# Long convolution packed into column and row tiles, with the sequence as weight and its result fetched by DMA

## The chip, the core and the metric

One core of one Trainium2 chip. The time is device microseconds for one execution, the median of three runs. Names used here: TensorE (PE; PEld are its weight loads), VectorE (DVE), ScalarE (ACT), GpSimd (POOL), SyncE (SP), which issues most DMAs. Arithmetic is in fp32. F32R is the format in which TensorE reads 4-byte values in one pass with reduced precision; the kernel gets full precision from it by splitting an operand into a high and a low part and adding three products.

## The reference

A block of two layers on x of 2 × 4096 × 256. The first normalises the rows, projects them to 3 × 256 channels, applies a 3-tap convolution along the sequence, and then a convolution as long as the sequence, whose filter is a sum of 16 decaying exponentials per channel:

```python
x2, x1, v = jnp.split(z_pre, 3, axis=1)
h = jnp.sum(residues[:, :, None] * jnp.exp(log_poles * t[None, None, :]), axis=1)
xv = x1 * v
yconv = jnp.fft.irfft(jnp.fft.rfft(xv, n=n) * jnp.fft.rfft(h, n=n)[None], n=n)[..., :Lc]
y = (yconv + xv * D_skip[None, :, None]) * x2
y = y.transpose(0, 2, 1) @ out_proj_w.T + u
zm = rmsnorm(y, post_norm_w)
return y + jax.nn.gelu(zm @ l1_w.T) * (zm @ l2_w.T) @ l3_w.T
```

The second layer is a feed-forward of width 1024 whose two weights get, per batch of 4096 rows, an update made from a few of its input rows.

## The kernel before

Three stages, each a block of its own per engine. The instructions of each engine stand in the order written; semaphores are the only link between engines.

**Stage A** (`phase_a`) takes 16 units of 512 rows: normalisation, projection, short convolution. It writes x2 to DRAM (`x2_scratch`) and leaves xv = x1·v, turned so that time within a chunk of 128 is the partition, in `seq` [time 128, channel 256, chunk 64] (`gate_rows`, L376). It also makes the first 128 filter taps per channel and writes them to `taps_scratch`. `scan_consts` (L254) makes the masks `own` and `later` on GpSimd.

**Stage B** (`phase_b`) is the long convolution, in 32 groups of 8 channels. Per group:

- TensorE `states_of`: the weighted sums of each chunk into 8 × 16 states. The weights are `collect`, exponentials of the poles; `seq` streams. Both are split into F32R parts by ScalarE (`gather`, L672 to L677) and VectorE (`low_parts`, L719), so three products of 512 columns (L749).
- VectorE: `inflow` masks and scales the sums (L729), and a scan over the chunks carries the states (L735, 512 columns), with ScalarE's `decay` (L681).
- TensorE: the part within a chunk is a product with a Toeplitz matrix of the taps, one per channel: the 128 × 128 matrix is the weight, the channel's 64 columns of `seq` stream, in plain fp32 (L762). The part from the earlier chunks is `spread` (L684) as weight and `state` streamed, 512 columns (L768), added in the same PSUM bank `ps_y`.
- ScalarE `take` (L693) copies the result back to `seq`, over its input.
- SyncE loads the Toeplitz matrices of a group straight from `taps_scratch` (512 KB, runs of 512 B) into one of two buffers. GpSimd meanwhile loads and splits the weights of stage C, one piece after another through one buffer `raw`.

TensorE's order is: sums of group g + 1, Toeplitz product of g, state product of g. The engines' steps run in a loop over pairs of groups (`run_steps`), with addresses in registers.

**Stage C** (`phase_c`) takes 32 units of 256 rows through output projection, MLP, feed-forward and norms, as a software pipeline. For the convolution's result, GpSimd copies a unit's two chunks out of `seq` (`copy_y`, L948), TensorE turns them by four transposes into `ps_rt` between blocks 2 and 3 of the MLP (`turn_y`), and VectorE multiplies by x2 there (`gate_y` part 0, L1117), then splits the product (`yt`) for the output projection. The same PSUM tile `ps_rt` serves the two other turns of a unit. TensorE's products are written through one helper, so its matmuls of C all have L1331 and its transposes L1341.

## Time and profile before

| | |
|---|---|
| median of 3 runs | 1200.15 us (1199.13 to 1202.2) |
| the profiled execution: its time, its span | 1203.2 us, 1201.5 us |
| TensorE busy, share of the span | 1123.1 us, 93% |
| VectorE, ScalarE, GpSimd busy | 957.5, 757.2, 325.9 us |
| stage A, B, C | to about 206, to about 326, to the end |
| mean granted clock of TensorE | 0.979 of full speed |
| moved by DMA | 80.72 MB, mean 67 GB/s |

A time in a row below is counted from the start of the span. Matmuls are pipelined, so the distance between two starts says more than the length of one. A count (x16) on a row of the timeline means that so many instructions were merged into it, and the row's time is from the first start to the last end.

### The profile page before, as it was taken

Reading aid. Unit: us, or ns where it says so; the run is one execution under the profiler, and the core shown is the slowest. Engines: PE = TensorE matmul, PEld = TensorE weight load, DVE = VectorE, ACT = ScalarE, POOL = GpSimd, SP = SyncE. Lnnn points to the kernel's source line nnn. Section 1 sums busy time; section 2 is a strip of 40 time slices with the busy share of each in tenths; the row PEclk is TensorE's granted clock in tenths of the full one; section 3 lists DMA queues with packets and bytes.
Section 4 is the critical chain, followed back from the end, with each engine's and each line's share of the span. In section 5 each row is a group of like instructions: output and inputs, shape, how many; then the busy total and the mean of one; then the engine's idle time right before and its main releaser. Section 6 shows DMA issues by size and latency. Waiting matters only on the chain.

```text
span 1201.5 us, 25905 instructions
## 1 busy us (share of the span) xinstructions
PE 1123.1 (93%) x9056; PEld 1079.9 (90%) x9056; DVE 957.5 (80%) x2375; ACT 757.2 (63%) x1697; POOL 325.9 (27%) x587
## 2 busy tenths in 40 slices
PE   3999998899868899999999999998999999999996
PEld 3889997678668899999999999997999999999996
DVE  5999997998647978877788878789788777888774
ACT  5878886677544656665566665566566655666643
POOL 5676663640011121112211122221211122211111
PEclk9999999999978899999999999998999999999999
DMA  3232322765432011111111111141111111111000
GB/s 115 79 115 77 100 71 72 238 180 157 132 114 71 27 37 45 45 45 46 36 36 51 39 45 45 37 141 36 36 45 45 45 45 37 37 45 45 28 19 27
DMA packets 90837, 80.72 MB, mean 67 GB/s; under 512 B 5040, under 2 KB 85584, under 8 KB 90720
## 3 DMA queue, kind: packets, MB, share of 16 engines
q1 hardware_dynamic: 89184, 76.76, 20.4%
q0 software_dynamic: 672, 2.39, 0.6%
q8 instruction: 68, 1.11, 0.4%
q14 instruction: 49, 0.40, 0.1%
q10 hardware_dynamic: 864, 0.05, 0.0%
HBM read 62.12 MB, written 17.07 MB: 66 GB/s over the span
## 4 chain that ended last, share of the span: by engine, by line
PE 51%; ACT 9%; issue 7%; DVE 5%; POOL 1%; ACTq 0%; POOLq 0%; DVEq 0%
PE ps_ring L1331 23%; PE ps_w L1331 13%; PE ps_m L1331 8%; PE ps_o L1331 3%; PE ps_rt L1341 3%; ACT gate L1021 2%; ACT frow L1028 2%; ACT pt_h L1015 2%; ACT ht_h L1040 1%; ACT hid L1043 1%; DVE base L1186 1%; POOL sc L953 1%; DVE ht_l L1108 1%; PE ps_m L1382 1%; DVE bn L1096 1%
## 5 line engine op out<-in xcount | busy, mean ns | idle before, releaser
L953 POOL TENSOR_TENSOR sc<-sc,neg_half 128x2 f32<-128x2 f32 x128 | 95.8, 749 | 673.2 <-DVE sc L1286 385.7
L1021 ACT ACTIVATE gate<-ps_ring 128x256 f32<-128x256 f32 x192 | 72.8, 379 | 168.1 <-PE ps_ring L1331 167.2
L1331 PE MATMUL ps_ring<-mt_h,wl_h 128*128 128x256 f32 x640 | 133.5, 291 | 6.4 <-ACT mt_h L1085 6.4
L1331 PE MATMUL ps_ring<-mt_l,wl_h 128*128 128x256 f32 x640 | 131.4, 287 | 6.7 <-DVE mt_l L1108 6.7
L1331 PE MATMUL ps_ring<-mt_h,wl_l 128*128 128x256 f32 x640 | 130.0, 285 | 0.0
L1043 ACT ACTIVATE hid<-ps_ring,b1s 128x256 f32<-128x256 f32 x256 | 111.5, 483 | 17.1 <-DVE ht_l L1108 17.0
L1134 DVE TENSOR_TENSOR prod<-ps_ring,gate 128x256 f32<-128x256 f32 x192 | 80.4, 419 | 46.1 <-ACT gate L1021 44.6
L1331 PE MATMUL ps_ring<-xt_h,we_h 128*128 128x256 f32 x512 | 106.1, 288 | 8.1 <-ACT hid L1043 5.8
L1331 PEld LDWEIGHTS ps_ring<-mt_h,wl_h 128*128 128x128 f32 x640 | 101.6, 197 | 7.7 <-ACT mt_h L1085 4.4
L1331 PEld LDWEIGHTS ps_ring<-mt_l,wl_h 128*128 128x128 f32 x640 | 101.7, 196 | 7.6 <-DVE mt_l L1108 7.6
L1108 DVE TENSOR_TENSOR ht_l<-hid,ht_h 128x256 fp32r<-128x256 f32 x256 | 100.8, 422 | 6.1 <-ACT hid L1043 1.7
L1331 PEld LDWEIGHTS ps_ring<-mt_h,wl_l 128*128 128x128 f32 x640 | 101.3, 196 | 0.0
L1331 PE MATMUL ps_ring<-xt_l,we_h 128*128 128x256 f32 x512 | 101.2, 279 | 0.0
L1331 PE MATMUL ps_ring<-xt_h,we_l 128*128 128x256 f32 x512 | 101.1, 278 | 0.0
L432 DVE SCALAR_TENSOR_TENSOR conv<-ps_z,sw,conv 128x512 f32<-128x512 f32 x128 | 92.1, 740 | 4.8 <-ACT conv L367 3.9
L1331 PEld LDWEIGHTS ps_ring<-xt_h,we_h 128*128 128x128 f32 x512 | 77.2, 188 | 14.7 <-ACT hid L1043 11.3
L1108 DVE TENSOR_TENSOR pt_l<-prod,pt_h 128x256 fp32r<-128x256 f32 x160 | 87.7, 548 | 1.1
L502 PE MATMUL ps_z<-zt_h,win_h 128*128 128x258 f32 x384 | 84.0, 300 | 2.8 <-DVE zt_l L427 2.7
L1000 ACT ACT_TABLE_LOAD x64 | 82.1, 1283 | 1.1
L502 PE MATMUL ps_z<-zt_h,win_l 128*128 128x258 f32 x384 | 78.2, 285 | 0.0
L502 PE MATMUL ps_z<-zt_l,win_h 128*128 128x258 f32 x384 | 78.2, 285 | 0.0
L1331 PEld LDWEIGHTS ps_ring<-xt_h,we_l 128*128 128x128 f32 x512 | 77.8, 188 | 0.0
(179 smaller groups left out, 3061.9 us busy)
## 6 DMA issues: line engine op xcount, KB each, us to landing
toep<-taps_scratch SPq DMA_DIRECT2D x32, 512.0 KB, 3.8
xa<-in_x SPq DMA_DIRECT2D x16, 512.0 KB, 4.6
x_scratch<-x2c SPq DMA_DIRECT2D x16, 512.0 KB, 3.5
x2s<-x_scratch SPq DMA_DIRECT2D x32, 256.0 KB, 2.9
xa_c<-in_x SPq DMA_DIRECT2D x32, 256.0 KB, 2.7
xb_c<-in_x SPq DMA_DIRECT2D x32, 256.0 KB, 2.7
out<-frow SPq DMA_DIRECT2D x32, 256.0 KB, 2.1
base<-in_w SPq DMA_DIRECT2D x8, 256.0 KB, 4.4
```

The source lines that it names most:

```text
L432: nc.vector.scalar_tensor_tensor(conv_of(m, u), tap_of(b, tap), sw[:, m, tap:tap + 1], conv_of(m, u), ALU.mult, ALU.add).then_inc(S[done], 1)
L502: mm = nc.tensor.matmul(slot(b)[:, a, 0:HALF + HALO], win_r[w][:, k, m * P:(m + 1) * P], zt[r][:, u % 2, k, cols], start=(j == 0), stop=(j ...
L953: nc.gpsimd.tensor_tensor(sc[:, to], sc[:, to], neg_half[:, 0, 0:CC], ALU.pow).then_inc(S[done], 1)
L1000: nc.scalar.activation(mark_act[:], neg_half[:, 0, 0:1], function)
L1015: nc.scalar.activation(high, src, ACT.Copy).then_inc(S["ph_done"], 1)
L1021: nc.scalar.activation(gate[rows_of, m % 2], ring[m % RING][rows_of, 0], ACT.Gelu_apprx_tanh).then_inc(S["gate_done"], 1)
L1028: nc.scalar.activation(frow[:, c], frow[:, c], ACT.Identity, scale=sc[:, 2, c:c + 1], bias=shift[:, 2, c:c + 1]).then_inc(S["f_norm"], 1)
L1043: nc.scalar.activation(hid[:, m % HIDS], block_of, ACT.Gelu, bias=b1s[:, m:m + 1]).then_inc(S["hid_done"], 1)
L1108: nc.vector.tensor_tensor(low, src, high.bitcast(F32), ALU.subtract).then_inc(S[done], 1)
L1134: nc.vector.tensor_tensor(product_views(m)[1], value, gated, ALU.mult).then_inc(S["prod_done"], 1)
L1331: mm = nc.tensor.matmul(out, lhs(a, kk), rhs(b, kk), start=(j == 0), stop=(closed and j == len(todo) - 1))
L1341: mm = nc.tensor.transpose(dst[:, b, chunk(c)], src[:, c, b * P:(b + 1) * P], ident[:])
```

## The change

- The layout of `seq` becomes [128, channel mod 128, channel half, chunk]: channels p and p + 128 lie side by side as a pair. Poles, residues and taps are put in the same order. A group is four pairs.
- Chunk sums: no split. For each pair a plain fp32 matmul with 32 weight columns writes its own 32 partitions of `ps_s` (column tiles of 32), 128 columns streamed. Both channels of a pair meet both channels' poles; `own` zeroes the wrong half, and `inflow`, `decay` and the scan have 256 columns in place of 512. One exponential makes `collect` for four groups.
- Toeplitz product: the sequence is the weight (64 columns), the Toeplitz matrix streams (128 columns). The two channels of a pair write partitions 0 to 63 and 64 to 127 (column tiles of 64). The result has the chunk as partition and time as column.
- State product: `state` is the weight (64 rows, 128 columns) and `spread` streams, in row tiles of 64 that write two banks.
- Three Toeplitz buffers in place of two; the poles come in two pieces (832 KB and 1 MB) in place of three; `raw` has two buffers; the loops are written out.
- Stage C fetches the result: for each unit four DMAs, each from one partition of `seq` (128 runs of 512 B) to the 128 partitions of `yin`. `copy_y` and `turn_y` go, and `gate_y` reads `yin`. SyncE asks for unit n + 2 once the gate of unit n + 1 has read the buffer, and ahead of the load of x2.

Stages A and B, cut:

```diff
+        yin = sb(whole, "yin", [P, KB, TC])
         mark = sb(whole, "mark", [P, 1])
...
-        seq = sb(whole, "seq", [P, D, COLS])
+        seq = sb(whole, "seq", [P, P, KB, COLS])
...
-                    sp.dma_start(taps_dram.rearrange("(k p) t -> p k t", p=P), taps[:]
+                    sp.dma_start(taps_dram.rearrange("(p k) t -> p k t", k=KB), taps[:]
...
+                nc.gpsimd.memset(own[:], 1.0).then_inc(v["bconst"], 1)
+                nc.gpsimd.memset(own_high[:], 1.0).then_inc(v["bconst"], 1)
+                nc.gpsimd.memset(later[:], 1.0).then_inc(v["bconst"], 1)
+                pool.wait_ge(v["bconst"], 5)
+                nc.gpsimd.memset(later[:, :, :, 0:1], 0.0).then_inc(v["bconst"], 1)
...
-                nc.scalar.activation(seq[:, j * P:(j + 1) * P, u * CA:(u + 1) * CA],
+                nc.scalar.activation(seq[:, :, j, u * CA:(u + 1) * CA],
...
         lpb = sb(ctx, "lpb", [P, (GROUPS - FIRST) * P])
         pole_chunk = sb(ctx, "pole_chunk", [P, GROUPS])
-        collect = sb(ctx, "collect", [P, 2, P])
-        collect_r = [sb(ctx, f"collect_{s}", [P, 2, P], F32R) for s in "hl"]
-        seq_r = [sb(ctx, f"seq_{s}", [P, 2, GC * COLS], F32R) for s in "hl"]
+        collect = sb(ctx, "collect", [P, 2, QUAD * P])
         spread = sb(ctx, "spread", [P, 2, CH])
-        decay = sb(ctx, "decay", [P, 2, 2 * GC * BC])
-        inflow = sb(ctx, "inflow", [P, 2, 2 * GC, BC])
-        state = sb(ctx, "state", [P, 2, 2 * GC * BC])
-        toep = sb(ctx, "toep", [P, 2, GC, CH])
-        raw = sb(ctx, "raw", [P, KB, FF])
+        decay = sb(ctx, "decay", [P, 2, 2 * KB * B * BC])
+        inflow = sb(ctx, "inflow", [P, 2, 2, KB * COLS])
+        state = sb(ctx, "state", [P, 2, 2, KB * COLS])
+        toep = sb(ctx, "toep", [P, TOEPS, GC, CH])
+        raw = sb(ctx, "raw", [P, 2, KB, FF])
         post = sb(ctx, "post", [P, KB])
-        ps_s = [ps(ctx, f"ps_s{i}", [P, 2 * GC, BC]) for i in range(2)]
-        ps_y = [ps(ctx, f"ps_y{i}", [P, 2 * GC * BC]) for i in range(2)]
...
+        ps_s = [ps(ctx, f"ps_s{i}", [P, KB * COLS]) for i in range(2)]
+        ps_y = [ps(ctx, f"ps_y{i}", [P, 2, 512]) for i in range(2)]
...
-            def load(g, par):
+            def load(g):
 
                 src = bass.AP(taps_dram.tensor, 2 * CH * GC * g, [[1, P], [2 * CH, GC], [1, CH]])
-                wait(sp, toep_mm, g - 1)
-                sp.dma_start(toep[:, par], src).then_inc(toep_in[par], 16)
+                wait(sp, toep_mm, g - TOEPS + 1)
+                sp.dma_start(toep[:, g % TOEPS], src).then_inc(toep_in[g % TOEPS], 16)
...
+            load(0)
+            load(1)
             load_poles(0)
-
-            def step(g, par, k):
-                if not (is_step(g) and g == 0) and valid(g + 1, GROUPS):
-                    load(g + 1, 1 - par)
-                if is_step(g) and g in (1, 2):
-                    load_poles(g)
-
-            run_steps(sp, step, plan)
+            load(2)
+            load_poles(1)
+            for g in range(3, GROUPS):
+                load(g)
             for i in range(2):
                 sp.wait_ge(v["x2_out"][i], 16 * UA // 2)
             sp.dma_start(v["x2s"][:], v["x2_dram"][:, :, 0:TC]).then_inc(v["x2_in"], 16)
+            sp.wait_ge(y_done, GROUPS)
             sp.wait_ge(v["x2_in"], 16)
 
...
+            def load(k, dst, src):
+                pool.dma_start(dst, src).then_inc(raw_in[k % 2], 16)
+
+            def load_l(k, w):
+                load(k, raw[:, k % 2], w.rearrange("(k p) f -> p k f", p=P))
+
+            raw_out = raw[:, 0, :, 0:D]
+            raw_l3 = flat(1)[:, 0:FULL * D].rearrange("p (m o) -> p m o", o=D)
+            raw_stack = raw[0:3 * REST, 0, 0, 0:D]
+            pool.dma_start(post[:], v["post_w"]).then_inc(post_in, 16)
+            load_l(0, v["l2_w"])
+            load_l(1, v["l1_w"])
+            pool.wait_ge(post_in, 16)
+            count = 0
+            for k, (dst, at) in enumerate(((v["wl2"], 0), (v["wl1"], REST))):
...
+                if k == 0:
+                    load(0, raw_out, v["out_w"].rearrange("(k p) o -> p k o", p=P))
+                else:
+                    load(1, raw_l3, v["l3_w"][0:FULL * P].rearrange("(m p) o -> p m o", p=P))
...
+                    for q in range(3):
+                        load(0, raw_stack[q * REST:(q + 1) * REST], v["l3_w"][FULL * P:])
...
+            def gather(q):
+
+                wait(act, s_mm, QUAD * (q - 1))
+                first = q * QUAD
+                if q == 0:
+                    nc.scalar.activation(collect[:, 0, 0:FIRST * P], lpb_first[:], ACT.Exp, scale=to_end[:, 0:1]
+                                         ).then_inc(collect_done, 1)
+                    act.wait_ge(poles_more[0], 16)
+                    nc.scalar.activation(collect[:, 0, FIRST * P:], lpb[:, 0:(QUAD - FIRST) * P], ACT.Exp,
+                                         scale=to_end[:, 0:1]).then_inc(collect_done, 1)
+                else:
+                    if (first - FIRST) * P + QUAD * P > pole_pieces[1]:
+                        act.wait_ge(poles_more[1], 16)
+                    at = (first - FIRST) * P
+                    nc.scalar.activation(collect[:, q % 2], lpb[:, at:at + QUAD * P], ACT.Exp,
+                                         scale=to_end[:, 0:1]).then_inc(collect_done, 1)
+
+            def powers(g):
+                wait(act, scan_done, g - 1)
+                nc.scalar.activation(decay[:, g % 2], later[:].rearrange("p a c j -> p (a c j)"), ACT.Copy,
+                                     scale=pole_chunk[:, g:g + 1]).then_inc(decay_done, 1)
+                wait(act, y_mm, g - 1)
+                nc.scalar.activation(spread[:, g % 2], ahead[:], ACT.Exp, scale=lpg[:, g:g + 1]
+                                     ).then_inc(spread_done, 1)
+
+            def take(g):
+                act.wait_ge(y_mm, g + 1)
+                nc.scalar.activation(seq[:, pairs_of(g)].rearrange("p (r a) k c -> p r (a k c)", r=2),
+                                     ps_y[g % 2][:, :, 0:2 * P], ACT.Copy).then_inc(y_done, 1)
+
             nc.scalar.activation(pole_chunk[:], lpg[:], ACT.Exp, scale=float(CH)).then_inc(pole_done, 1)
+            gather(0)
             act.wait_ge(pole_done, 1)
...
+            powers(0)
+            gather(1)
+            for g in range(GROUPS):
                 if valid(g + 1, GROUPS):
-                    powers(g + 1, 1 - par)
+                    powers(g + 1)
                 if valid(g - 1, GROUPS):
-                    take(g - 1, 1 - par)
-
-            run_steps(act, step, plan)
-            take(GROUPS - 1, 1)
+                    take(g - 1)
+                if g % QUAD == 0 and 2 <= g // QUAD + 1 < GROUPS // QUAD:
+                    gather(g // QUAD + 1)
+            take(GROUPS - 1)
...
-            def low_parts(g, par):
-                dve.wait_ge(high_done, 2 * (g + 1))
-                for low, src, high in ((seq_r[1], seq[:, bass.ds(g * GC, GC), :].rearrange("p h c -> p (h c)"),
-                                        seq_r[0]), (collect_r[1], collect[:, par], collect_r[0])):
-                    nc.vector.tensor_tensor(low[:, par], src, high[:, par].bitcast(F32), ALU.subtract
-                                            ).then_inc(low_done, 1)
-
-            low_parts(0, 0)
-            low_parts(1, 1)
...
+            for g in range(GROUPS):
                 dve.wait_ge(s_mm, g + 1)
                 wait(dve, scan_done, g - 1)
-
-                nc.vector.scalar_tensor_tensor(inflow[:, par, :, 1:BC], ps_s[par][:, :, 0:BC - 1],
-                                               rg[:, bass.ds(g, 1)], own[:, :, 0:BC - 1],
+                ends = ps_s[g % 2][:, 0:KB * COLS - 1].unsqueeze(1).broadcast_to([P, 2, KB * COLS - 1])
+                nc.vector.scalar_tensor_tensor(inflow[:, g % 2, :, 1:], ends, rg[:, g:g + 1],
+                                               own[:].rearrange("p a c j -> p a (c j)")[:, :, 0:KB * COLS - 1],
                                                ALU.mult, ALU.mult).then_inc(inflow_done, 1)
                 dve.wait_ge(inflow_done, g + 1)
                 dve.wait_ge(decay_done, g + 1)
                 wait(dve, y_mm, g - 1)
-                nc.vector.tensor_tensor_scan(state[:, par], decay[:, par],
-                                             inflow[:, par].rearrange("p c j -> p (c j)"), 0.0,
+                nc.vector.tensor_tensor_scan(state[:, g % 2].rearrange("p a c -> p (a c)"), decay[:, g % 2],
+                                             inflow[:, g % 2].rearrange("p a c -> p (a c)"), 0.0,
                                              ALU.mult, ALU.add).then_inc(scan_done, 1)
...
-            def states_of(g, par):
-                pe.wait_ge(low_done, 2 * (g + 1))
+            def states_of(g):
+                pe.wait_ge(collect_done, 1 if g < FIRST else 2 + g // QUAD)
                 wait(pe, inflow_done, g - 1)
-                for j, (a, b) in enumerate(((0, 0), (0, 1), (1, 0))):
-                    mm = nc.tensor.matmul(ps_s[par][:].rearrange("p c j -> p (c j)"),
-                                          collect_r[a][:, par], seq_r[b][:, par],
-                                          start=(j == 0), stop=(j == 2))
+                for j in range(PAIRS):
+                    at = (g % QUAD) * P + j * 2 * STATES
+                    mm = nc.tensor.matmul(ps_s[g % 2][j * 2 * STATES:(j + 1) * 2 * STATES],
+                                          collect[:, g // QUAD % 2, at:at + 2 * STATES],
+                                          seq[:, g * PAIRS + j].rearrange("p k c -> p (k c)"),
+                                          start=True, stop=True)
                 mm.then_inc(s_mm, 1)
...
-            def step(g, par, k):
+            def out_of(g, j):
+                return ps_y[g % 2][:, j // 2, (j % 2) * P:(j % 2 + 1) * P]
+
+            states_of(0)
+            for g in range(GROUPS):
                 if valid(g + 1, GROUPS):
-                    states_of(g + 1, 1 - par)
-                pe.wait_ge(toep_in[par], 16 * (k + 1))
+                    states_of(g + 1)
+                pe.wait_ge(toep_in[g % TOEPS], 16 * (g // TOEPS + 1))
                 wait(pe, y_done, g - 1)
-                for c in range(GC):
-                    mm = nc.tensor.matmul(ps_y[par][:, c * COLS:(c + 1) * COLS], toep[:, par, c],
-                                          seq[:, bass.ds(g * GC + c, 1), :].rearrange("p h c -> p (h c)"),
-                                          start=(c == 0), stop=False, skip_group_check=True)
+                for j in range(PAIRS):
+                    for k in range(KB):
+                        mm = nc.tensor.matmul(out_of(g, j)[k * HALF:(k + 1) * HALF],
+                                              seq[:, g * PAIRS + j, k], toep[:, g % TOEPS, KB * j + k],
+                                              start=(j % 2 == 0), stop=False, skip_group_check=True)
                 mm.then_inc(toep_mm, 1)
                 pe.wait_ge(spread_done, g + 1)
                 pe.wait_ge(scan_done, g + 1)
-                nc.tensor.matmul(ps_y[par][:], spread[:, par], state[:, par], start=False, stop=True,
-                                 skip_group_check=True).then_inc(y_mm, 1)
-
-            run_steps(pe, step, plan)
+                for a in range(2):
+                    for r in range(2):
+                        rows = slice(r * HALF, (r + 1) * HALF)
+                        mm = nc.tensor.matmul(out_of(g, 2 * r + a), state[rows, g % 2, a], spread[rows, g % 2],
+                                              start=False, stop=(a == 1), skip_group_check=True)
+                mm.then_inc(y_mm, 1)
```

Stage C and the order of the channels, cut:

```diff
+            def load_y(n):
+                for k in range(KB):
+                    for c in range(CC):
+                        row = k * COLS + n * CC + c
+                        sp.dma_start(yin[:, k, c * CH:(c + 1) * CH],
+                                     seq[row:row + 1].rearrange("p i k c -> p i (k c)")).then_inc(S["y_in"], 16)
+
+            load_y(0)
...
                 if valid(n + 2, UC):
+                    sp.wait_ge(S["yf_done"], n + 2)
+                    load_y(n + 2)
                     sp.wait_ge(S["yl_done"], n + 2)
                     sp.dma_start(x2s[:], x2_dram[:, :, (n + 2) * TC:(n + 3) * TC]).then_inc(S["x2_in"], 16)
...
-            def copy_y(n):
-
-                wait(pool, S["yt_mm"], n)
-                nc.gpsimd.tensor_copy(ys[:], seq[:, :, n * CC:(n + 1) * CC].rearrange("p h c -> p c h")
-                                      ).then_inc(S["y_copied"], 1)
-
...
-                    dve.wait_ge(S["yt_mm"], n + 1)
+                    dve.wait_ge(S["y_in"], 16 * KB * CC * (n + 1))
                     dve.wait_ge(S["x2_in"], 16 * (n + 1))
-                    back = ps_t[:].rearrange("p b (c t) -> p (b c) t", t=CH)[:, :, ::-1]
+                    back = yin[:].rearrange("p b (c t) -> p (b c) t", t=CH)[:, :, ::-1]
...
-            def turn_y(n):
-                pe.wait_ge(S["y_copied"], n + 2)
-                wait(pe, S["zl_done"], n)
-                transpose_unit(ps_t, ys).then_inc(S["yt_mm"], 1)
-
...
-                pe.wait_ge(S["yf_done"], n + 1)
+                wait(pe, S["zl_done"], n)
...
-                pe.wait_ge(S["yf_done"], min(u + 3, UC))
...
+    grouped = np.arange(D).reshape(KB, GROUPS, GC // KB).transpose(1, 2, 0).reshape(D)
```

## Rows read from the trace of the kernel before

**Rows 1.** windows by stage: each engine busy (instructions), granted clock, DMA share, GB/s

```profile
226.00:326.00 100.00, 96.73 (x599) 76.76 (x598) 84.16 (x108) 68.67 (x162) 22.93 (x20) 1.00 0.56 165
...
332.00:343.00 11.00, 6.38 (x29) 5.86 (x29) 1.98 (x4) 5.14 (x12) 0.72 (x1) 0.50 0.74 237
...
430.00:790.00 360.00, 356.85 (x3063) 353.98 (x3063) 287.13 (x828) 222.95 (x536) 70.52 (x126) 1.00 0.14 45
```

**Rows 2.** timeline, TensorE in stage B: start us, us, engine, line, operation

```profile
227.16 1.08 PE L768 MATMUL ps_y<-state,spread 128*128 128x512 f32 x2
...
264.61 0.80 PE L749 MATMUL ps_s<-seq_h,collect_h 128*128 128x512 f32 x1
...
265.48 0.39 PE L749 MATMUL ps_s<-seq_h,collect_l 128*128 128x512 f32 x1
265.71 1.89 PE L762 MATMUL ps_y<-seq,toep 128*128 x16
267.44 1.08 PE L768 MATMUL ps_y<-state,spread 128*128 128x512 f32 x2
267.95 0.79 PE L749 MATMUL ps_s<-seq_h,collect_h 128*128 128x512 f32 x1
...
323.68 1.08 PE L768 MATMUL ps_y<-state,spread 128*128 128x512 f32 x2
```

**Rows 3.** timeline around the transposes of one unit in stage C

```profile
599.50 0.40 PE L1331 MATMUL ps_ring<-mt_l,wl_h 128*128 128x256 f32 x2
...
599.73 0.60 PE L1341 MATMUL ps_rt<-ident,ys 128*128 128x128 f32 x4
...
600.40 0.39 PE L1331 MATMUL ps_ring<-mt_h,wl_l 128*128 128x256 f32 x2
...
600.69 1.10 DVE L1108 TENSOR_TENSOR pt_l<-prod,pt_h 128x256 fp32r<-128x256 f32 x1
...
602.67 0.39 PE L1331 MATMUL ps_ring<-mt_l,wl_h 128*128 128x256 f32 x2
602.89 0.39 PE L1331 MATMUL ps_ring<-mt_h,wrest_h 128*64 128x256 f32 x2
603.12 0.39 PE L1331 MATMUL ps_ring<-mt_l,wrest_h 128*64 128x256 f32 x2
...
625.32 0.60 PE L1341 MATMUL ps_rt<-ident,ys 128*128 128x128 f32 x4
```

**Rows 4.** groups of stage B (busy us, mean ns | idle before); one timeline row

```profile
L735 DVE TENSOR_TENSOR_SCAN state<-decay,inflow 128x512 f32<-128x512 f32 x32 | 40.2, 1257 | 1.1
...
L729 DVE SCALAR_TENSOR_TENSOR inflow<-ps_s,rg,own 128x496 f32<-128x496 f32 x32 | 23.3, 730 | 9.9 <-PE ps_s L749 9.9
L681 ACT ACTIVATE decay<-later,pole_chunk 128x512 f32<-128x512 f32 x32 | 22.6, 708 | 0.0
L674 ACT ACTIVATE seq_h<-seq 128x512 fp32r x26 | 16.0, 615 | 0.0
...
L693 ACT ACTIVATE seq<-ps_y 128x512 f32 x26 | 15.0, 576 | 0.0
...
L684 ACT ACTIVATE spread<-ahead,lpg 128x128 f32<-128x128 f32 x32 | 12.8, 401 | 26.7 <-PE ps_y L768 26.6
...
220.23 2.25 DVE L735 TENSOR_TENSOR_SCAN state<-decay,inflow 128x512 f32<-128x512 f32 x1
```

**Rows 5.** one microsecond of stage B with the DMA engines full

```profile
230.00:231.00 1.00, 1.00 (x11) 1.00 (x11) 0.96 (x2) 1.00 (x4) 0.00 (x0) 1.00 0.96 314
```

**Rows 6.** DMA issues: count, KB each, median us to landing

```profile
toep<-taps_scratch SPq DMA_DIRECT2D x32, 512.0 KB, 3.8
...
x2s<-x_scratch SPq DMA_DIRECT2D x32, 256.0 KB, 2.9
```

**Rows 7.** timeline at the start of stage C

```profile
325.66 0.39 SPq L903 DMA_DIRECT2D xa_c<-in_x  x1
...
327.19 0.69 DVE L1117 TENSOR_TENSOR x2s<-ps_rt,x2s 128x512 f32<-128x512 f32 x1 [5.82 <-PE ps_rt L1341]
```

167 lines of the change are left out of this document (49 added, 118 removed).

## Prediction

> **What bounds the kernel now.** TensorE is busy for 93% of the span, so I read the busy time by stage first [rows 1]. The long convolution (stage B) lies at 206 to 326 us, and the row-wise stage C fills the rest. From 226 to 326 TensorE is busy 96.7 of 100 us, in steady C 356.9 of 360. The reader should see three more things there. The DMA engines are at 0.56 in B and only at 0.14 in C. ScalarE has 69 of 100 us of work in B. And TensorE's granted clock is 1.00 (2.4 GHz) in both, and 0.50 (1.2 GHz) at the seam at 332 to 343, behind a stretch in which it stood still.
>
> Then I read one group of 8 channels of B in order of time [rows 2]. A group takes 267.95 − 264.61 = 3.34 us, and its parts follow one another. The 16 records of the Toeplitz product go from 265.71 to 267.44: 1.73, so 0.108 each. The state product starts at 267.44 and has two records of 512 columns. The record behind it shows 0.79 where its twin shows 0.39, so its first 0.40 were waiting, and the state product held the engine until 268.35: 0.91 us for 1024 columns, 0.89 ns a column. The three records of the chunk sums have the remaining 0.70. A record of these, in F32R, starts 0.23 ahead of the next one (265.48, 265.71) for 512 columns: 0.45 ns a column. So a plain fp32 product is two records, each at twice the time per column of an F32R one. 1.73 + 0.91 + 0.70 is all of the 3.34: B is TensorE's own work, with no wait of size. Over the last 28 groups the mean is (323.68 − 227.16)/28 = 3.45, since some waited.
>
> In C the result of B costs TensorE four transposes per unit of 256 rows. The pair of matmuls ahead of them starts at 599.50, the second pair after them at 600.40. Between lie two pairs' own time, 603.12 − 602.67 = 0.45 us [rows 3]. 0.90 − 0.45 leaves 0.45 us for the transposes.
>
> **Stage B, part by part.** *TensorE.* A record of 128 plain fp32 columns costs 128 × 0.89 ns = 0.114 us. After the change a group has 4 matmuls of 128 columns for the chunk sums (8 records), 8 for the Toeplitz product (16) and 4 for the states (8): 32 records, 3.65 us if nothing overlaps. That is 0.31 more than now, since the Toeplitz product streams 128 columns where it streamed 64. So everything hangs on whether the tiles run beside each other, and no row of before shows two tiles at once. The nearest are the 128*64 matmuls of C: alone in their half of the array they start 0.23 a pair, like the full ones, and the change of shape costs nothing that can be seen (602.67, 602.89, 603.12) [rows 3]. The bounds are 3.65 (no overlap) and, with four tiles at once for the sums and two for the rest, 0.23 + 0.91 + 0.46 = 1.6.
>
> I choose between them like this. The two records of one fp32 matmul share a tile and must follow each other. If records start in program order, the second of one tile runs with the first of the next, which is a factor of two for every part, four tiles or not: 1.83. Weight loads come on top. A Toeplitz record of today streams 64 columns, 0.057 us, but they start 0.108 apart, so a load of 128 weight columns sets their pace. The state product of after has 8 such loads, 0.87 in place of 0.46. That gives 2.24; I take 2.2 us a group.
>
> *VectorE* loses both low parts; its inflow shrinks from 496 to 254 columns and its scan from 512 to 256. Even unchanged the two are 0.73 + 1.26 = 2.0 [rows 4], halved about 1.2. *ScalarE* loses the high parts; decay (0.71, on half the columns), spread (0.40), take (0.58) and a quarter of one exponential on 512 columns (0.61/4) are at most 1.84 [rows 4]. Both are below 2.2.
>
> *DMA.* Each group still reads 512 KB of Toeplitz rows. With the engines full, one microsecond shows 314 GB/s [rows 5], so 524 kB take 1.7 us. A load took 3.8 us to land [rows 6]. With three buffers three periods must hold that and about 0.9 of Toeplitz product: 1.6 us a group. The DMA floor of 1.7 is near, yet below 2.2.
>
> *The start of B.* ScalarE now waits, in order, for an 832 KB piece of poles before it makes the first decay and spread, where 192 KB sufficed. Queued by then are two Toeplitz loads, that piece, and GpSimd's two 672 KB loads, which now leave together: 3.3 MB, over 10 us at 0.31 MB/us. Behind the waiting ScalarE stand VectorE's first scan, TensorE's first state product and all later groups. But the queue itself sets the fourth group: four Toeplitz loads, 1.9 MB of poles and GpSimd's 1.4 MB are 5.4 MB, 17 us from 207, which ends at 224, and the fourth group's state product of before started at 227.16 [rows 2]. I cost the start at nothing, with −2 to +3. GpSimd's splits once held a scan for 2.25 us [rows 4]; with shorter groups that reaches TensorE. I add 2 us.
>
> B: 28 × (3.45 − 2.2) − 2 = 33 us saved. At the DMA floor 28 × 1.75 − 2 = 47.
>
> **Stage C.** Taking the transposes out gives 0.45 us in each of 31 units, 13.9 us. They lie on the path that sets the end, for TensorE hardly waits here and what it does wait for (ScalarE's gates and hidden layer) follows from its own blocks. A low part at 600.69 takes 1.10 us beside GpSimd's copy [rows 3], more than the product needs alone; that is VectorE's time, which is not the path in the steady part. I do not add it.
>
> What comes in is four SyncE DMAs of 64 KB per unit, each from one partition to 128. In the steady part they leave when the gate of the unit before has read the buffer and have nearly a period, 625.32 − 599.73 = 25.6 us [rows 3], to land. That period is their cover. Behind them on SyncE's queue are the loads of x2, the store of the result and the two loads of x, each for the next unit; I take them as covered while the four take less than half a period. The first transfer has no cover: the first gate starts at 327.19 today, 1.5 us after the stage's first issue at 325.66 [rows 7]. Below: two or three issues of 0.4 us and 2.9 us, as 256 KB of x2 took to land [rows 6]; together 2 more than now. Above: if one partition gives only what one of 16 DMA engines gets at 314 GB/s, 19.6 GB/s, 64 KB take 3.3 us and four 13.4, 12 more than now. The row is as far from this as can be, so I take the middle, 7.
>
> By "SBUF — State Buffer", Door 1, of the Trainium skill, one SBUF port passes about 27 GB/s to DMA, and neighbouring partitions share a port. Four loads of 2.4 us would be an estimate of 9.6, and this term 9 in place of 7. No trace here has a load from one partition.
>
> **The sum.** −33 − 14 + 7 = −40. The profiled execution took 1203.2 (span 1201.5), so 1163. It lies 3.05 above the median of the runs: 1160. Stage A changes in the stride of its writes to seq (runs of four elements, as before) and in some GpSimd constants made once; I cost both at nothing, with GpSimd's idle time in A as cover, and at 2 us without it.
>
> **The rivals.** *Tiles overlap only in part* (0.18). A Toeplitz weight load of 64 columns is half of 0.108. If such loads are not hidden behind the neighbour's stream, 16 add 0.87 to 2.24, and half of that if every second one is. A group is then 2.7 to 3.1, B saves 19 to 8, the total is −26 to −15: about 1180. Against it: the full-width loads of C hide, since a pair of 256 columns takes no more than its columns at 0.45 ns. For it: the Toeplitz records of today are paced by loads.
> By "TensorE: Matmul & The Clock Gate", Part 3, of the Trainium skill, a weight load overlaps running matmuls only where the row groups differ, and column tiles share theirs; the rows of C do not agree with it in that plain form, and no row of before has two tiles.
>
> *No overlap at all* (0.12), the case on the other side. The place is the Toeplitz step. A group becomes 3.65 and 0.05 of gaps: 32 × 0.36 = 12 us slower. With −14 and +7 that is +5: 1205. It decides from 3.5 us a group on. For it: nothing in this trace shows two tiles at once. Against it: only that their operands and results lie apart.
>
> *The single-partition loads become C's bound* (0.08). When four take over 25 us the gate waits in every unit; at 6.7 us each the 1.5 us a unit eats all that B gave, which is 1200. The upper bound above is half of that.
>
> *Packed, as forecast*, has 0.62 and a range of its own, 1141 to 1171: below, B at the DMA floor and the first transfer at +2 (−47 − 14 + 2 = −59); above, 2.4 us a group and the first at +12 (−27 − 14 + 12 = −29). The full range is 1140 to 1190: it takes in most of the partial case and leaves out the last two. What a measurement tells from no change is 0.3%, 3.6 us. Faster are the packed and the partial case and half of the loads' case: 0.83. Within 0.3% are 0.05 of what is left, where the small terms decide. Slower: 0.12.
>
> **What would show it.** Right: groups of B 2.2 us apart; Toeplitz records of the two halves less than 0.1 apart, with the clock at 1.00; units of C shorter by 0.45; the first gate of C 4 to 14 us after the stage begins. Wrong: records 0.11 apart and a period of 3.7; TensorE waiting in every group for toep (then the DMA queue is the bound, not the array) or for state; the clock at 0.50 within B, for each record then takes twice its time; or the gate waiting for yin in every unit.

## The result, and the profile after

| | before | after |
|---|---|---|
| median of the runs | 1200.08 us (1199.13 to 1202.2, 4 runs) | 1170.78 us (1164.41 to 1173.5, 4 runs) |
| the profiled execution: its time, its span | 1203.2, 1201.5 us | 1170.21, 1168.5 us |
| mean granted clock | 0.979 | 0.966 |

The ratio is 0.9746, with a 95% interval of 0.9704 to 0.9788: faster, by 29 us, where 40 were forecast (1160, range 1140 to 1190). Four runs of the changed kernel lie 9 us apart, those of before 3.

Windows by stage come first, as for before [rows 1]; the cuts are the first Toeplitz load (start of stage B), the first load of stage C and its first gate.

```profile
0.00:210.61 210.61, 182.38 (x1408) 173.66 (x1408) 176.29 (x309) 158.19 (x275) 130.18 (x278) 0.98 0.26 85
210.61:299.44 88.83, 70.25 (x1024) 52.80 (x1024) 42.22 (x66) 46.65 (x106) 26.84 (x26) 0.87 0.84 248
299.44:310.04 10.60, 0.00 (x0) 0.00 (x0) 0.00 (x1) 0.00 (x0) 0.00 (x0) 0.68 0.64 54
310.04:1168.50 858.46, 815.86 (x6848) 804.70 (x6848) 661.77 (x1936) 516.68 (x1228) 128.18 (x256) 0.98 0.34 57
```

Before, stage B began at 206.5 and the first issue of C stood at 325.66, the first gate at 327.19 [rows 7]. So the four stretches went from 206.5, 119.1, 1.5 and 874.3 us to 210.6, 88.8, 10.6 and 858.5: +4.1, −30.3, +9.1, −15.8, which is the −33.0 between the two spans. The whole of B before, in the same columns:

```profile
206.50:325.66 119.16, 111.40 (x672) 88.34 (x672) 101.19 (x130) 81.26 (x193) 32.23 (x26) 0.97 0.62 184
```

The DMA share of B rose from 0.62 to 0.84, and TensorE, which stood still for 7.8 of 119.2 us before, does so for 18.6 of 88.8.

One group of B in order of time, on TensorE (compare [rows 2]):

```profile
251.92 0.43 PE L736 MATMUL ps_s<-seq,collect 128*32 128x128 f32 x8
252.27 1.09 PE L753 MATMUL ps_y<-toep,seq 128*64 128x128 f32 x16
253.30 0.71 PE L762 MATMUL ps_y<-spread,state 64*128 64x128 f32 x8
253.94 0.43 PE L736 MATMUL ps_s<-seq,collect 128*32 128x128 f32 x8
```

By starts, the chunk sums take 0.35 us, the Toeplitz products 1.03 and the state products 0.64: 2.02 us for 32 records. That is 0.044, 0.064 and 0.080 us a record, where a lone record of 128 such columns was worth 0.114. The tiles do run beside each other. But 28 such periods would be 57 us, and from the fourth group's state product (235.05) to the last one's (297.67) are 62.6: 2.24 a group. What TensorE waited for from 226 to 300, by the view of waits (waited for: us in total, times, longest):

```profile
PE ps_y L762 <- DVE state L725: 9.7, 1, 9.7
PEld ps_y L753 <- DMA toep<-taps_scratch: 6.2, 7, 2.8
...
PE ps_y L753 <- DMA toep<-taps_scratch: 4.3, 4, 2.5
```

The second and third rows are the Toeplitz loads, in seven groups; over the whole stage TensorE's matmuls waited for them for 6.8 us, in five. The first row is the start of the stage, here on ScalarE and VectorE:

```profile
222.77 0.40 ACT L672 ACTIVATE collect<-lpb,to_end 128x128 f32<-128x128 f32 x1 [11.36 <-DMA lpb<-in_lp_flat]
223.08 0.49 ACT L683 ACTIVATE decay<-later,pole_chunk 128x256 f32<-128x256 f32 x1
...
223.67 2.93 DVE L725 TENSOR_TENSOR_SCAN state<-decay,inflow 128x256 f32<-128x256 f32 x1 [10.93 <-ACT decay L683]
```

ScalarE waits 11.36 us for 832 KB of poles, and everything behind it with it; the first state product comes 16.1 us after the first load. Over these 16 us the windows show the DMA engines full:

```profile
210.61:226.75 16.14, 3.06 (x32) 2.20 (x33) 3.65 (x5) 3.24 (x9) 8.66 (x9) 0.52 1.01 342
```

At the start of C, SyncE's queue and the first gate (compare [rows 7]), and then the loads of the steady part (count, KB each, median us to landing; compare [rows 6]):

```profile
299.44 4.83 SPq L898 DMA_DIRECT2D yin<-seq  x4
304.31 1.34 SPq L902 DMA_DIRECT2D xa_c<-in_x  x1
...
310.04 0.69 DVE L1104 TENSOR_TENSOR x2s<-yin,x2s 128x512 f32<-128x512 f32 x1 [14.05 <-DMA yin<-seq]
```

```profile
out<-frow SPq DMA_DIRECT2D x32, 256.0 KB, 5.8
yin<-seq SPq DMA_DIRECT2D x124, 64.0 KB, 6.3
x2s<-x_scratch SPq DMA_DIRECT2D x31, 256.0 KB, 7.2
```

The four transfers hold the gate for 10.6 us and move 262 kB in it, 24.7 GB/s with issue and landing counted in. In the steady part each takes 6.3 us to land, and whatever is queued behind them takes longer too (x2 7.2 for 2.9). Yet the gate waits for them in no later unit: they are hidden there, as forecast.

### The profile page after: what moved, and what is told of

It reads as the page before. It is cut to its first block, busy times and chain, and to the rows that moved or that the text cites. A ratio compares the mean times of both kernels' runs of the same rounds, so it can differ in the third digit from the quotient of the medians.

```text
span 1168.5 us, 25495 instructions
## 1 busy us (share of the span) xinstructions
PE 1068.5 (91%) x9280; PEld 1031.2 (88%) x9280; DVE 880.3 (75%) x2311; ACT 721.5 (62%) x1609; POOL 285.2 (24%) x560
## 3 DMA queue, kind: packets, MB, share of 16 engines
q8 instruction: 74, 1.21, 0.4%
## 4 chain that ended last, share of the span: by engine, by line
PE 51%; ACT 8%; issue 7%; DVE 5%; DMA 1%; SPq 1%; POOL 1%; ACTq 0%; DVEq 0%; POOLq 0%
PE ps_ring L1318 24%; PE ps_w L1318 13%; PE ps_m L1318 8%; PE ps_o L1318 3%; PE ps_rt L1328 2%; ACT gate L1008 2%; ACT frow L1015 2%; ACT pt_h L1002 2%; ACT ht_h L1027 1%; ACT hid L1030 1%; DVE base L1173 1%; DMA yin<-seq 1%; POOL sc L948 1%; PE ps_m L1364 1%; DVE bn L1083 1%
## 5 line engine op out<-in xcount | busy, mean ns | idle before, releaser
L1318 PE MATMUL ps_ring<-mt_h,wl_h 128*128 128x256 f32 x640 | 130.5, 286 | 6.4 <-ACT mt_h L1072 6.4
L1121 DVE TENSOR_TENSOR prod<-ps_ring,gate 128x256 f32<-128x256 f32 x192 | 80.9, 421 | 48.1 <-ACT gate L1008 46.1
L1318 PEld LDWEIGHTS ps_ring<-xt_l,we_h 128*128 128x128 f32 x512 | 77.8, 188 | 0.0
```

What stands on the lines that cost most here:

```text
L1121: nc.vector.tensor_tensor(product_views(m)[1], value, gated, ALU.mult).then_inc(S["prod_done"], 1)
L1318: mm = nc.tensor.matmul(out, lhs(a, kk), rhs(b, kk), start=(j == 0), stop=(closed and j == len(todo) - 1))
```

## The experiments

A note on scatter. Each kernel below but the last was run once, and its stages were read from the trace of that run. Where a stage's code was untouched, its length still differed: stage A (constants in one place) ended at 207.9 to 210.6 in ten runs, mean 209.2; stage B with its own loads took 85.5 to 90.6 in four; C from the first gate took 856.3 to 863.8 in twelve, mean 860.1 (in three of these the four transfers of a unit were changed, nothing else). So a stage is compared with these spreads, and a total only where it moves by more.

### Do the tiles overlap, and what paces a record?

**Neighbours in the same half.** The loops over channel halves and pairs change places:

```
-                for j in range(PAIRS):
-                    for k in range(KB):
+                for k in range(KB):
+                    for j in range(PAIRS):
```

Expected: 

> The eight Toeplitz products of a group are issued in another order: the four of the first channel half, then the four of the second, so that (but for one pair) each matmul follows one into the same 64 PSUM partitions; nothing else is changed, and the result is the same. Theory (a matmul overlaps the one before it only when the two write different column tiles): a group's Toeplitz products go from 1.03 us to about 1.7 us (16 records of about 0.107), the period of a steady group from 2.03 to about 2.7 us, stage B and the kernel about 20 us longer, near 1190 us. Rival (the 0.064 us a record is what a 64-column stationary costs anywhere, and the tiles' neighbourhood does nothing): the period stays 2.03 us and the time 1171 us within 3 us.

Measured: 1181.27 us, 10.5 above the median of the changed kernel. TensorE's timeline:

```profile
262.13 1.58 PE L753 MATMUL ps_y<-toep,seq 128*64 128x128 f32 x16
263.64 0.72 PE L762 MATMUL ps_y<-spread,state 64*128 64x128 f32 x8
264.29 0.43 PE L736 MATMUL ps_s<-seq,collect 128*32 128x128 f32 x8
```

The same 16 records take 1.51 us (263.64 − 262.13) in place of 1.03, 0.094 each. Nothing but the order changed, so the gain comes from neighbours in different column tiles. (With the tile, the order of the PSUM columns and banks changes too; no run separates the two.) The size was less than expected (1.51, not 1.7; the period 2.51, not 2.7), and the stage grew by 8.4 us to 97.2, not by the 15 that 31 × 0.48 would make. The stalls for Toeplitz loads shrank in return, from 6.8 us to 3.9, which is the first sign that TensorE was no longer alone in setting the pace.

**All chunk sums in one quarter.** From group 2 on the four sums of a group go to the first 32 partitions:

```
-                    mm = nc.tensor.matmul(ps_s[g % 2][j * 2 * STATES:(j + 1) * 2 * STATES],
+                    q = j if g < 2 else 0
+                    mm = nc.tensor.matmul(ps_s[g % 2][q * 2 * STATES:(q + 1) * 2 * STATES],
```

Expected: 

> From group 2 on the four chunk sums of a group all go to the same 32 PSUM partitions instead of four different ones, so that the states of three of four channel pairs are wrong; the count of instructions and the work are unchanged. Theory (column tiles overlap): the four sums go from 0.35 us to about 0.85 us (8 records of 0.107), the period from 2.03 to about 2.5 us, the kernel about 12 us longer. Rival (the sums are cheap for their 32 columns alone): no change, 0.35 us and 2.03 us.

Measured: 1183.9 us; the sums of a group:

```profile
262.16 1.06 PE L737 MATMUL ps_s<-seq,collect 128*32 128x128 f32 x8
263.15 1.09 PE L754 MATMUL ps_y<-toep,seq 128*64 128x128 f32 x16
```

0.99 us for eight records against 0.35: a factor of 2.8 for four tiles, where two tiles gave 1.5 (0.094 against 0.064). Part of it may be something else: here the four products also write the same addresses, one over the other, and 0.124 us a record is more than the 0.114 of a lone one. The period is 2.66 in 29 of 31 cases, without one stall. That more than two tiles can be under way at once rests on the changed kernel's own 0.044 against 0.114, a factor of 2.6; the forecast's "factor of two for every part, four tiles or not" is too low for the sums (0.46 forecast, 0.35 measured).

**Half the columns.** From group 2 on each Toeplitz product streams 64 of its 128 columns (`0:cols` with `cols = CH // 2` on output and Toeplitz block).

Expected: 

> From group 2 on each Toeplitz product streams only 64 of its 128 columns, so that half of every chunk's output lacks its Toeplitz part; the instructions, their stationaries and all loads stay. Theory (with overlap, each Toeplitz record is paced by its columns: two tiles share a stream of 0.107 us): the eight products go from 1.03 to about 0.55 us, the group's period from 2.03 to about 1.75 us, where the DMA traffic of 1.7 us a group begins to hold it. Rival (the weight loads, 64 columns each and unchanged, pace the records at 0.064 us): the products stay at about 1.0 us and the period at 2.03 us.

Measured: 1170.03 us: no gain at all. The products fell to 0.61 us a group (262.57 to 263.18), 0.038 a record, and the shortest periods to 1.61. So columns pace the record, not its 64-column weight load. But the stage did not follow: 86.1 us, within the spread of the unchanged stage. Here are 40 us of B, first of the changed kernel and then of this one (each engine's busy time, granted clock, DMA share, GB/s):

```profile
250.00:290.00 40.00, 38.34 (x606) 28.93 (x607) 22.28 (x38) 26.79 (x61) 0.00 (x0) 1.00 0.87 245
```

```profile
250.00:290.00 40.00, 32.42 (x620) 23.81 (x618) 22.86 (x40) 27.34 (x64) 0.00 (x0) 0.98 0.95 250
```

By the starts of the state products a group takes 2.13 us in the first (251.27 to 289.59, 18 periods) and 2.03 in the second (249.69 to 288.26, 19). TensorE's work fell by 15%, the groups came 5% faster, and the DMA share went to 0.95. In this window Toeplitz blocks are the only large loads, and 524 kB at 250 GB/s are 2.1 us. The forecast's floor of 1.7 had used 314 GB/s, read in a single microsecond of before [rows 5]. That is too short a stretch: in this window of the half-column run, cut into 40 slices of 1 us, single ones have from 67 to 342 GB/s.

```profile
GB/s 178 295 67 246 251 214 281 229 337 296 245 205 263 259 281 226 214 231 342 286 272 285 266 270 243 161 323 101 121 315 254 276 194 342 239 308 236 304 239 308
```

Other loads were moving in that microsecond as well, and they may reach a higher rate: the first 16 us of B, with poles and weights in them, had 342 GB/s.

### What bounds stage B now?

**Half the bytes.** The direct test of that reading: a Toeplitz block is loaded for four of eight channels, and all products use these.

```
-                src = bass.AP(taps_dram.tensor, 2 * CH * GC * g, [[1, P], [2 * CH, GC], [1, CH]])
+                src = bass.AP(taps_dram.tensor, 2 * CH * GC * g, [[1, P], [2 * CH, GC // 2], [1, CH]])
...
-                                              seq[:, g * PAIRS + j, k], toep[:, g % TOEPS, KB * j + k],
+                                              seq[:, g * PAIRS + j, k], toep[:, g % TOEPS, (KB * j + k) % (GC // 2)],
```

Expected: 

> Each Toeplitz block is loaded for four of its eight channels (256 KB instead of 512, in the same 512-byte packets), and all eight products use these four, so that half of the convolution's taps are wrong; the number of instructions and the work of every engine stay. Theory (what is left of stage B above 2.03 us a group is the bytes of its loads: half the product time changed nothing, and other orders of the loads only 2 to 3 us): no waits for Toeplitz blocks from group 3 on, a period of 2.03 us throughout, the first output a few us earlier, stage B 76 to 79 us against 88.8, the kernel at 1159 us. Rival (the stalls are GpSimd's and VectorE's shared work or the clock, not the DMA): stage B stays at 86 to 89 us.

Measured: 1159.7 us, and stage B 78.4 us (88.8 in the changed kernel, 85.5 to 90.6 in its repeats). Windows, columns as above:

```profile
230.00:250.00 20.00, 19.50 (x314) 14.72 (x306) 14.08 (x20) 14.57 (x33) 17.27 (x16) 1.00 0.67 180
250.00:270.00 20.00, 19.95 (x320) 15.13 (x320) 11.78 (x21) 13.70 (x32) 0.14 (x1) 1.00 0.49 130
```

TensorE is full there, 28 of 31 periods are 2.02 to 2.15, and the granted clock stays at 1.00 from 230 on. In the changed kernel it was 0.87 from 230 to 250, where TensorE stood still for a Toeplitz block and the next groups' records took longer:

```profile
244.69 1.46 PE L753 MATMUL ps_y<-toep,seq 128*64 128x128 f32 x16 [2.49 <-DMA toep<-taps_scratch]
246.08 1.23 PE L762 MATMUL ps_y<-spread,state 64*128 64x128 f32 x8
```

GpSimd's folding of the weights went on as before (17.27 of 20 us), so it is not what held the steady part of B. The Toeplitz loads are: half of them is worth about 10 us of stage B. Of these, 4.4 us come before the first state product (11.7 us after the first load, for 16.1), and half of that is a scan which did not meet GpSimd's work this time, as is worked out below. The run halves the number of 512-byte pieces together with the bytes, so it does not tell which of the two the DMA engines' time goes by.

**The order of the loads.** Three kernels move the side loads of B and leave their bytes alone: the poles in four pieces with a small one first; the same, and GpSimd's second weight load held until the first matrix is folded; and poles in eight pieces with five weight loads paced by the outputs. Their cores:

```
-        pole_pieces = (0, 13 * P, (GROUPS - FIRST) * P)
+        pole_pieces = (0, P, 5 * P, 17 * P, (GROUPS - FIRST) * P)
```
```
             pool.dma_start(post[:], v["post_w"]).then_inc(post_in, 16)
+            pool.wait_ge(post_in, 16)
             load_l(0, v["l2_w"])
-            load_l(1, v["l1_w"])
-            pool.wait_ge(post_in, 16)
...
                 if k == 0:
+                    load_l(1, v["l1_w"])
```
```
-            for g in range(3, GROUPS):
+            for g in range(1, GROUPS):
                 load(g)
+                if g % QUAD == QUAD - 1 and g // QUAD + 2 < GROUPS // QUAD:
+                    load_poles(g // QUAD + 2)
```

Expected, poles in four: 

> The poles for the chunk-end factors are loaded in four pieces (1, 4, 12 and 12 groups) instead of two (13 and 16), the first ahead of the first Toeplitz block and the last after the tenth block. Theory (the first exponentials wait for 832 KB, 11.4 us, of which one group's 64 KB are needed): ScalarE starts 6 to 8 us earlier, the first output of B moves from 226.8 to about 220 us, and the kernel is 5 to 7 us shorter, 1165 us, if the transfers that were ahead of it do not give it back in the stall at group 5. Rival (stage B is bound at its start by bytes: 2.3 MB of poles, Toeplitz blocks and weights in any order): the first output comes earlier but group 8 does not, and the kernel stays within 2 us of 1171 us.

Expected, with the weights held: 

> As the run with the poles in four pieces, and GpSimd's second weight load (640 KB) waits until the first matrix is folded, as it does in the kernel before. Theory (bytes at the start of B are the second cause): the stall of 5 us at group 5 shrinks as well, another 2 to 3 us, 1162 us. Rival (that load fits in the gaps of the Toeplitz traffic): no gain over the run with the poles alone.

Expected, all paced: 

> Stage B's side loads are spread over it: the poles come in eight pieces, each just ahead of the four groups that use it, and GpSimd's five weight loads wait for outputs 2, 7, 11, 15 and 18; bytes and instructions are otherwise the same. What the runs so far show: with half the Toeplitz columns the period of a group falls to 1.61 us, but stage B does not get shorter, at a DMA share of 0.96 and 247 GB/s, so the Toeplitz blocks alone need about 2.1 us a group. Theory (stage B is now bound by the bytes, about 20 MB at 250 GB/s, in whatever order): the first output comes 8 us earlier than in the changed kernel, stalls are spread, and the stage (first Toeplitz load to first load of C) is 83 to 86 us against 88.4, the kernel at 1166 to 1169 us. Rival (the stalls were a matter of order, and TensorE's 2.03 us a group bound the rest): the stage falls to 32 x 2.03 + 9 = 74 to 77 us, the kernel to 1158 us.

Measured: 1168.79, 1167.33 and 1162.9 us, and stage B 87.2, 85.3 and 85.9 us. With the poles in four the first state product came 9.1 us after the first load (217.06 − 207.96) instead of 16.1, and most of that was given back: of the 7.0 us, 2.9 are left at the twelfth group and 1.7 at the last. Its waits for Toeplitz blocks, against 6.8 us in five groups in the changed kernel over the same window:

```profile
PE ps_y L755 <- DMA toep<-taps_scratch: 14.0, 8, 5.3
```

One of the three stages lies well inside the unchanged one's spread (85.5 to 90.6), two at its low end, so a gain of 2 us may be there and is not shown. The expected 5 to 7 us of an earlier start are refuted: what starts earlier waits for bytes later. The paced kernel's 1162.9 is no proof of more, for its C took 856.4, the low end of the spread too.

### One partition as source

**128 source partitions.** The same bytes into the same places, but `seq[:, row]` instead of `seq[row:row + 1]`, so that stage C gets other channels' data.

Expected: 

> The four transfers that fetch a unit's convolution result read 128 partitions (512 bytes of each) instead of one partition (64 KB of it); they carry the same bytes into the same places, but not the wanted channels, so stage C computes with wrong data. Theory (one source partition is read through one port, and 256 KB take about 10 us through it): from the first issue to the first gate of stage C 10.6 us become about 4 us, the landing of one transfer 6.3 us becomes 3 us, the kernel 6 to 7 us shorter, 1164 us. Rival (the time is the 512-byte packets and the cost of issuing, whatever the source): the start of C stays at 10 us and the kernel within 2 us of 1171 us.

Measured: 1162.08 us. The first gate came 4.5 us after the first issue (304.04 − 299.51), against 10.6, and in the steady part (columns as above):

```profile
out<-frow SPq DMA_DIRECT2D x32, 256.0 KB, 2.2
yin<-seq SPq DMA_DIRECT2D x120, 64.0 KB, 1.9
x2s<-x_scratch SPq DMA_DIRECT2D x30, 256.0 KB, 3.1
```

The store of the result and the load of x2 are back at what before showed for them (2.1 and 2.9), and the four transfers themselves take 1.9. The source's one partition costs 6 us at the start of C, and the longer landings behind it.

**Rows apart.** The four transfers in the order of partitions 0, 64, 1, 65 instead of 0, 1, 64, 65:

```
-                for k in range(KB):
-                    for c in range(CC):
+                for c in range(CC):
+                    for k in range(KB):
```

Expected: 

> The four transfers of a unit are issued in the order of chunks, then halves, so that neighbours read partitions 64 apart instead of one apart; nothing else is changed. Theory (each source partition has a port of its own rate, and transfers of one queue run one after another): the start of C moves by less than 1 us, unless partitions 0 and 1 share a port and 0 and 64 do not, in which case neighbours overlap and the 10.6 us become about 6 us. Rival (the issue of the four on the queue, 4.8 us, and what follows it set the start): no change at all.

Measured: 1166.84 us; from first issue to first gate 7.75 us in place of 10.60, and a landing of 4.8 us in place of 6.3. With 262 kB that is 33.8 GB/s. What the DMA engines moved from first issue to first gate, in 40 slices, first in the changed kernel (0.27 us a slice) and then here (0.19):

```profile
GB/s 0 0 0 0 14 91 25 25 29 33 29 21 23 29 29 25 21 19 29 29 29 41 93 77 31 27 25 14 27 27 31 31 72 147 149 114 103 158 267 207
```

```profile
GB/s 0 0 0 0 0 85 29 26 32 16 29 40 26 26 16 32 77 93 82 61 50 61 45 58 24 40 37 37 53 32 108 169 153 119 90 159 233 259 275 174
```

In the changed kernel the slices from the seventh to the 32nd have 27 GB/s in the mean without the two at 93 and 77. With the rows apart the rate is 27 for ten slices and 54 in the mean of the next fourteen, with other loads mixed in. Neighbouring partitions hinder each other's transfers, distant ones do not, or less. The total agrees, though 4 us are within what it scatters.

By "SBUF — State Buffer", Door 1, of the Trainium skill, partitions 0 to 3 share a port and 64 to 67 have another, at about 27 GB/s a port. These two runs agree: 27 GB/s in the slices when neighbours on one port follow each other, more when the two ports take turns.

### The constants in stage A

The constants for the scan are built in seven pieces, one in each unit:

```
-                if n == 4:
-                    scan_consts()
+                if 4 <= n < 11:
+                    scan_consts(n - 4)
```

Expected: 

> GpSimd builds the constants of the scan in seven pieces, one in each unit from the fifth to the eleventh of stage A, instead of all between two units; the instructions are the same. Theory (3.8 us of GpSimd in one place hold up the tap products, TensorE idles for 3 us and loses its clock): the last store of stage A, 210.6 us at the start of B, comes about 3.6 us earlier, near 207 us, and the kernel is 3 to 4 us shorter, 1167 us. Rival (the lost 4 us come from elsewhere, and GpSimd's work costs the same wherever it is): B starts at 210 us and the kernel takes 1171 us.

Measured: 1167.04 us; B began at 205.40, 3.8 us ahead of the mean of the ten runs with the constants in one place. TensorE at the place in question, first in the changed kernel, then here:

```profile
82.17 1.12 PE L482 MATMUL ps_x<-ident,xv 128*128 128x128 f32 x4 [3.14 <-POOL xv L318]
...
83.51 0.63 PE L498 MATMUL ps_z<-zt_h,win_l 128*128 128x258 f32 x2
83.94 0.63 PE L498 MATMUL ps_z<-zt_l,win_h 128*128 128x258 f32 x2
```

```profile
79.52 0.63 PE L487 MATMUL ps_x<-ident,xv 128*128 128x128 f32 x4 [0.37 <-ACT seq L377]
...
80.23 0.40 PE L503 MATMUL ps_z<-zt_h,win_l 128*128 128x258 f32 x2
80.47 0.41 PE L503 MATMUL ps_z<-zt_l,win_h 128*128 128x258 f32 x2
```

A wait of 3.14 us for GpSimd became 0.37, and the pairs behind it start 0.24 apart instead of 0.43. The granted clock over the next six microseconds, by windows, says why: 0.50 (1.2 GHz) behind the wait of 3.14 us, 1.00 (2.4 GHz) without it.

```profile
82.00:88.00 6.00, 5.83 (x27) 5.84 (x28) 1.48 (x4) 1.26 (x2) 3.01 (x6) 0.50 0.01 3
```

```profile
79.50:86.00 6.50, 6.48 (x54) 6.39 (x55) 5.82 (x10) 5.54 (x10) 4.73 (x13) 1.00 0.10 37
```

The two rows are the changed kernel and this run; before the wait, from 76 to 78.5, the changed kernel's clock was 1.00 as well. The total is 3.7 us below the median, but B (85.5) and C (863.8) lie at opposite ends of their spreads in this run, so it proves nothing by itself. The run with all together, in which B began at 204.96, is the second to show the gain.

### All together

The last kernel has the constants spread, the paced loads, the rows apart, and one thing more: for the first unit the pairs of groups 0 to 27 are fetched in B's tail, behind the last Toeplitz load, and only 16 pairs after it.

```
+            sp.wait_ge(y_done, Y_EARLY)
+            for k in range(KB):
+                for c in range(CC):
+                    row, pairs = k * COLS + c, Y_EARLY * PAIRS
+                    sp.dma_start(v["yin"][0:pairs, k, c * CH:(c + 1) * CH],
+                                 seq[row:row + 1, 0:pairs].rearrange("p i k c -> p i (k c)")
+                                 ).then_inc(v["y_early"], 16)
```

Expected: 

> All that paid, together, the computation complete: GpSimd's constants spread over seven units of stage A, the side loads of stage B spread over it, the first unit's result fetched for 112 of 128 channel pairs in stage B's tail, and the four transfers of a unit in the order that reads distant partitions. Theory (the losses are apart from each other and add up): 3.8 us in A, 3 us in B, and 7 us at the start of C (the first gate 3 to 4 us after the last output's transfers are issued, against 10.6), so 1157 us, ratio to the kernel before 0.964. Rival (the early fetch takes DMA time from the last Toeplitz blocks, or one source partition is slow for these as well): C starts only 3 us earlier, 1161 to 1164 us.

Measured: 1155.85 us (1155.39 to 1157.75, 4 runs) beside 1201.59 of before (7 runs); ratio 0.9622 (0.9603 to 0.964). It beats the changed kernel by 15 us by the medians, and the two intervals do not meet. B began at 204.96. The early transfers, the rest, and the first gate:

```profile
284.20 3.76 SPq L601 DMA_DIRECT2D yin<-seq  x4
290.77 2.76 SPq L917 DMA_DIRECT2D yin<-seq  x4
...
294.99 0.69 DVE L1125 TENSOR_TENSOR x2s<-yin,x2s 128x512 f32<-128x512 f32 x1 [7.87 <-DMA yin<-seq]
```

The gate comes 4.2 us after the stage's first issue, B took 85.8 us, C the usual 859.4. So against the profiled execution of the changed kernel: 5.7 us in A, 3.0 in B (within its spread), 6.4 at the start of C, −0.9 in the rest.

## Why the prediction was right, point by point

- **The overlap and the period of a group: right, by two errors that cancel.** Forecast were 2.2 us, TensorE's own work; measured are 2.24 over the last 28 groups, of which TensorE's work is 2.02. Its parts were forecast as 0.46, 0.91 and 0.87 and measured as 0.35, 1.03 and 0.64. The sums overlap by more than two. The state products, which were thought to be paced by loads of 128 weight columns at 0.108, run at 0.080 a record; no run says what sets that. The Toeplitz records came out above a plain factor of two (0.064, not 0.057).
- **"The DMA floor of 1.7 is near, yet below 2.2": the step that failed.** The floor is 2.0 to 2.1, as the run with half the columns shows (2.03 in 40 us at a DMA share of 0.95, 2.15 over the last 28 groups), and the one with half the bytes confirms that the loads make it. It fills the place of the part of the pacing by loads that was not there; that the two come to the same 2.2 is luck. A forecast with 2.0 us for TensorE and the 1.7 would have saved 38.6 us in B, 8 more than measured.
- **The start of B at nothing (−2 to +3).** The fourth group's state product came 24.4 us after the first load, 20.6 before: +3.8. Of these, 2.3 are the next term, so the start itself is +1.5, within its bounds. The poles' wait is real, 11.36 us on ScalarE, but most of what its removal gave was lost again by the twelfth group: what is late is bytes, 342 GB/s at a share of 1.01 from the first load on.
- **GpSimd's contention, +2.** Right, at 2.3. VectorE's first scan stands right ahead of the first state product. It took 2.93 us (223.67 to 226.60) while GpSimd subtracted; in the run with half the bytes it met no subtraction and took 0.69:

```profile
223.17 2.89 POOL L628 TENSOR_TENSOR wl_l<-raw,wl_h 128x1280 fp32r<-128x1280 f32 x1
```

```profile
220.47 0.69 DVE L725 TENSOR_TENSOR_SCAN state<-decay,inflow 128x256 f32<-128x256 f32 x1 [9.00 <-ACT decay L683]
```

  That is 2.2 us on the path. A second scan of 2.33 us made one period 2.11 in place of 2.02. Stage B as a whole: the period of 2.24 saves 33.9 us (28 × 1.21), the start takes 3.8, which makes 30.1 of the 30.3 measured; forecast were 35 and 2.
- **The transposes, −13.9.** C from its first gate is 15.8 shorter in the two profiles, and 14.2 by the mean of twelve (860.1). The gates of steady units, before and after:

```profile
448.34 0.68 DVE L1117 TENSOR_TENSOR x2s<-ps_rt,x2s 128x512 f32<-128x512 f32 x1
...
755.97 0.68 DVE L1117 TENSOR_TENSOR x2s<-ps_rt,x2s 128x512 f32<-128x512 f32 x1
```

```profile
452.71 0.68 DVE L1104 TENSOR_TENSOR x2s<-yin,x2s 128x512 f32<-128x512 f32 x1
...
755.87 0.68 DVE L1104 TENSOR_TENSOR x2s<-yin,x2s 128x512 f32<-128x512 f32 x1
```

  Over these twelve units one takes 25.64 us and then 25.26, 0.37 less; from the first gate to the last it is 0.49 a unit, where 0.45 were forecast. The size is right. That it is the transposes alone is argued and not shown: GpSimd's copies went with them, and no run puts either back.
- **The first transfer, +7 (bounds +2 to +12).** Measured +9.1. The mechanism was right, its size 2 us off; the chosen middle had no row behind it. The prediction's other estimate, worked out from the 27 GB/s of "SBUF — State Buffer", Door 1, of the Trainium skill, was nearer. Its sum is off by one, though: four loads of 2.4 us are 9.6, and less the 1.5 of before the term is 8, not 9. The slices above show that rate, 27 GB/s.
- **Steady loads hidden.** Right: of 32 gates one waits for the transfers, the first.
- **Stage A at nothing, "and at 2 us without" cover.** Wrong: +4.1 in the profile, +2.7 in the mean. The cover named was GpSimd's idle time, but the constants (3.8 us, from 77.0 to 80.9) stand in its program ahead of a product that TensorE waits for, and the clock was at 0.50 for six microseconds behind the pause. For before there is one profile, so its own scatter in A is not known.
- **The rivals.** No overlap is refuted (0.064 a record, 0.094 with neighbours in one tile). Partial overlap named 2.7 to 3.1 us a group; not seen. The loads as C's bound: 6.3 us each to land, near the 6.7 from which it was to decide, yet the four overlap in time and need 10.6 together in a unit of some 25. The landing time of one was no measure of the four.

The sum by stages: forecast 0, −33, +7, −14; measured +4.1, −30.3, +9.1, −15.8. The first three missed by 2 to 4 us on the same side and the last by 2 on the other, which makes −33 of the −40. The rest of the 11 us between 1160 and 1171 is that the profiled execution of before lay 3 us above its median, and that of after 0.6 below.

## What to carry to other kernels

Pack small matmuls so that neighbours in program order write different column tiles; the order of two loops was worth 0.48 us in 2.0. When one engine's work falls by 40%, recompute every other floor from rows with the same kind of load, and over tens of microseconds: the 314 GB/s read in one microsecond with mixed transfers did not hold for the Toeplitz blocks, which moved at 250. And an engine's idle time is cover only if nothing that others wait for stands behind the new work in its program: cut it into pieces, or put it where its queue ends.
